# Inverse softmax sums by way of DRAM instead of TensorE transposes, in an attention and feed-forward kernel

## The reference

```python
cq = rms_norm(x @ w_qa.T, q_a_ln_w)
q = (cq @ w_qb.T).reshape(b, s, H, DQ).transpose(0, 2, 1, 3)      # 16 heads of 128 + 64 (rope)
ckv = x @ w_kva.T                                                # 128 latent + 64 rope
kv = (rms_norm(ckv[..., :128], kv_a_ln_w) @ w_kvb.T)...           # k_nope, v
scores = einsum('bhqd,bhkd->bhqk', q_full, k_full) * scale        # causal mask
attn = softmax(scores.astype(float32), axis=-1)
out = einsum('bhqk,bhkd->bhqd', attn, v).transpose(0, 2, 1, 3).reshape(b, s, H * DV) @ w_o.T
x = layernorm(x + out)
x = layernorm(x + x @ (w_ffn * scale_w[:, None]).T + bias)
```

## Time and profile before

| | us |
|---|---|
| median of 3 runs (1714.79 to 1720.11) | 1716.27 |
| the profiled execution, its own time | 1716.44 |
| its span | 1714.7 |
| PE busy | 1679.9 (98%) |
| DVE busy | 1380.5 (81%) |
| ACT busy | 1120.8 (65%) |
| POOL busy | 979.7 (57%) |

### The profile page before, as it was taken

One profiled execution on the slowest core, in us unless ns is written; L12 is line 12 of the kernel. 1 busy time (PEld: TensorE's weight loads), 2 busy tenths in 40 slices (PEclk: granted clock), 3 DMA queues, 4 the chain that ended last, 5 costly groups with the idle time before them and its releaser, 6 DMA issues.

```text
span 1714.7 us, 28541 instructions
## 1 busy us (share of the span) xinstructions
PE 1679.9 (98%) x8789; PEld 1395.8 (81%) x8789; DVE 1380.5 (81%) x2493; ACT 1120.8 (65%) x2128; POOL 979.7 (57%) x937
## 2 busy tenths in 40 slices
PE   7999999999999999999999999999999999999997
PEld 5567888888888888888888888888888888888775
DVE  3665788888888887878788888888888888888984
ACT  3564676666666676666677666766667777676774
POOL 4333465565555555655566555555556665556785
PEclk9999999999999999999999999999999999999999
DMA  7984322212321412223211413123123111111422
GB/s 204 367 330 136 105 68 62 87 56 88 110 80 37 144 36 81 69 80 117 81 62 44 142 50 92 51 80 114 62 66 105 56 57 62 50 44 44 136 92 80
DMA packets 112175, 164.03 MB, mean 96 GB/s; under 512 B 13600, under 2 KB 83488, under 8 KB 109984
## 3 DMA queue, kind: packets, MB, share of 16 engines
q1 hardware_dynamic: 105296, 125.86, 22.9%
q0 software_dynamic: 4864, 16.26, 3.0%
q10 hardware_dynamic: 1872, 20.19, 2.9%
HBM read 101.19 MB, written 61.08 MB: 95 GB/s over the span
## 4 chain that ended last, share of the span: by engine, by line
PE 89%; POOL 3%; DVE 3%; issue 2%; DMA 1%; ACT 1%; DVEq 0%; SPq 0%; ACTq 0%; POOLq 0%
PE rows L1464 35%; PE bank L1494 7%; PE bank L1497 7%; PE bank L1495 7%; PE rows L1527 7%; PE rows L1427 5%; PE bank L1527 3%; PE rows L392 2%; PE rows L1440 2%; PE bank L1427 2%; PE bank L1484 2%; PE bank L1440 1%; POOL split_p L1730 1%; PE rows L1473 1%; PE rows L1505 1%
## 5 line engine op out<-in xcount | busy, mean ns | idle before, releaser
L1730 POOL TENSOR_TENSOR split_p<-pool,split_p 128x512 fp32r<-128x512 f32 x544 | 703.3, 1294 | 503.2 <-ACT split_p L1618 503.1
L1464 PE MATMUL rows<-q_c,key_c 128*128 128x512 f32 x1632 | 477.0, 400 | 1.4 <-DVE top L1858 1.4
L1606 ACT COPY pool<-rows 128x512 f32<-128x512 f32 x480 | 281.8, 587 | 227.3 <-PE rows L1464 226.6
L1858 DVE TENSOR_TENSOR top<-rows,top 128x512 f32<-128x512 f32 x420 | 288.6, 687 | 124.5 <-ACT pool L1606 121.0
L1873 DVE TENSOR_TENSOR pool<-bank,pool 128x512 f32<-128x512 f32 x544 | 369.7, 680 | 19.8 <-PE bank L1484 19.8
L1611 ACT ACTIVATE pool<-pool 128x512 f32<-128x512 f32 x544 | 345.9, 636 | 18.1 <-DVE pool L1873 17.1
L1618 ACT CAST split_p<-pool 128x512 fp32r<-128x512 f32 x544 | 333.2, 612 | 16.7 <-PE bank L1497 16.7
L1464 PE MATMUL rows<-q_pe,key_pe 128*128 128x512 f32 x1088 | 337.1, 391 | 0.4 <-DMA q_pe<-pe_dram 0.4
L1885 DVE TENSOR_TENSOR bank<-bank,pool 128x512 f32<-128x512 f32 x480 | 330.9, 689 | 0.0
L1464 PEld LDWEIGHTS rows<-q_c,key_c 128*128 128x128 f32 x1632 | 288.0, 189 | 50.0 <-DVE top L1858 5.0
L1464 PEld LDWEIGHTS rows<-q_pe,key_pe 128*128 128x128 f32 x1088 | 204.2, 188 | 46.2 <-DMA q_pe<-pe_dram 0.9
(11 more groups left out here) (193 smaller groups left out, 2101.9 us busy)
## 6 DMA issues: line engine op xcount, KB each, us to landing
q_pe<-pe_dram SPq DMA_DIRECT2D x128, 128.0 KB, 2.6
y_dram<-y SPq DMA_DIRECT2D x62, 256.0 KB, 2.1
cq<-cq_dram SPq DMA_DIRECT2D x19, 768.0 KB, 4.9
y<-y_dram SPq DMA_DIRECT2D x48, 256.0 KB, 3.0
pe_dram<-by_sin SPq DMA_DIRECT2D x32, 256.0 KB, 2.1
pe_dram<-by_cos SPq DMA_DIRECT2D x32, 256.0 KB, 2.2
cq_more<-cq_dram SPq DMA_DIRECT2D x10, 768.0 KB, 4.9
table<-table_dram SPq DMA_DIRECT2D x56, 128.0 KB, 2.7
```

Source lines behind the costliest of these rows:

```text
L1464: mm = pe.matmul(by_head(out), k, q, start=(z == 0), stop=(z == 4))
L1606: nc.scalar.copy(slot(n), SCORES[n % N_SCORES]).then_inc(scores_copied, 1)
L1730: nc.gpsimd.tensor_tensor(split_p[:, n % 2, 1, :], slot(n), stored(split_p[:, n % 2, 0, :]), ALU.subtract).then_inc(p_lo, 1)
L1858: nc.vector.tensor_tensor(out, SCORES[n % N_SCORES], slot(number(it, 0)) if t == 1 else out, ALU.max).then_inc(scores_maxed, 1)
```

## The change

`by_transfer(it)` picks 52 of the 64 query tiles: all but the last six and those six others whose next but one tile ends fewer than 8 slots after them (it 1, 5, 17, 21, 33 and 37). For these, `spread_sum` is gone. In its place SyncE stores `inv_sum` to a DRAM row of 512 numbers, head by head (`store_inv`, 128x4 elements, each element on its own in DRAM), waits for the store to land, and loads the row with one DMA onto all 128 partitions (`load_inv`, 128x512 floats), into one of two buffers. `normalise` multiplies by that SBUF row instead of the PSUM bank and moves from one slot after e + 3 to e + 7, `y` from e + 5 to e + 8. The buffers take the room of two ring tiles, so the ring goes from 24 to 22.

```diff
-RING = 24
+RING = 22
...
+def by_transfer(it):
+    return it + 6 < N_ITER and last_value(it + 2) - last_value(it) >= 8
...
-        yield e + 3, USE_AT, ("spread_sum", it)
-        yield e + 5, USE_AT, ("y", it)
+        if by_transfer(it):
+            yield e + 2, COPIES, ("store_inv", it)
+            yield e + 3, COPIES, ("load_inv", it)
+            yield e + 7, READ, ("normalise", it)
+            yield e + 7, READ, ("o_hi", it)
+            yield e + 7, READ, ("o_lo", it)
+            yield e + 8, USE_AT, ("y", it)
+        else:
+            yield e + 3, USE_AT, ("spread_sum", it)
+            yield e + 5, USE_AT, ("y", it)
...
+            def store_inv(it):
+                sp.wait_ge(inv_done, it + 1)
+                sp.dma_start(m.inv_dram[it].rearrange("(h p) -> p h", h=HG), inv_sum[it % 2],
+                             allow_slow_non_contiguous=True).then_inc(inv_stored[TRANSFERS[it] % 2], 16)
+            def load_inv(it):
+                n = TRANSFERS[it]
+                if n >= 2:
+                    sp.wait_ge(normalised, [o for o in TRANSFERS if TRANSFERS[o] == n - 2][0] + 1)
+                sp.wait_ge(inv_stored[n % 2], 16 * (n // 2 + 1))
+                sp.dma_start(inv_rows[:, n % 2, :], m.inv_dram[it].rearrange("(a n) -> a n", a=1).broadcast_to([P, P * HG])
+                             ).then_inc(inv_loaded[n % 2], 16)
...
             def normalise(it):
-                dve.wait_ge(sum_spread, it + 1)
                 dve.wait_ge(out_copied, it + 1)
+                if by_transfer(it):
+                    n = TRANSFERS[it]
+                    dve.wait_ge(inv_loaded[n % 2], 16 * (n // 2 + 1))
+                    nc.vector.tensor_tensor(o_sum[:, it % 2, :], inv_rows[:, n % 2, :], o_sum[:, it % 2, :], ALU.mult
+                                            ).then_inc(normalised, 1)
+                    return
+                dve.wait_ge(sum_spread, 1 + sum(not by_transfer(o) for o in range(it)))
```

More of the change, by code:

```diff
@@ L89, in __init__ @@
         self.small = sb("small", [P, 64])
-        self.pool = sb("pool", [P, RING * 512])
+        self.pool = sb("pool", [P, (RING + 2) * 512])
         self.cq_dram = nc.dram_tensor("cq_dram", (NCH, P, 2 * KR * 512), F32, kind="Internal").ap()
@@ L111, in __init__ @@
         self.cq_loaded = [ctx.enter_context(nc.semaphore(f"cq_loaded{n}")) for n in range(3)]
+        self.inv_dram = nc.dram_tensor("inv_dram", (G * NT, P * HG), F32, kind="Internal").ap()
         self.y_dram = nc.dram_tensor("y_dram", (NT, P, HID), F32, kind="Internal").ap()
@@ L734, in last_value @@
     return VALUE_SLOT[FIRST[it + 1] - 1]
+def by_transfer(it):
+    return it + 6 < N_ITER and last_value(it + 2) - last_value(it) >= 8
+TRANSFERS = {}
+for it in range(N_ITER):
+    if by_transfer(it):
+        TRANSFERS[it] = len(TRANSFERS)
 def window_slot(s, j):
@@ L917, in waits_for @@
         if it >= 2:
-            yield ("spread_sum", it - 2)
+            yield ("normalise", it - 2) if by_transfer(it - 2) else ("spread_sum", it - 2)
+    elif what == "store_inv":
+        yield ("reduce_sum", it)
+    elif what == "load_inv":
+        yield ("store_inv", it)
+        for other in TRANSFERS:
+            if TRANSFERS[other] == TRANSFERS[it] - 2:
+                yield ("normalise", other)
     elif what == "spread_sum":
@@ L922, in waits_for @@
         yield ("copy_out", it)
-        yield ("spread_sum", it)
+        yield ("load_inv", it) if by_transfer(it) else ("spread_sum", it)
     elif what == "o_hi":
@@ L1098, in sem @@
             return ctx.enter_context(nc.semaphore(name))
-        ring = m.pool[:, :].rearrange("p (r n) -> p r n", r=RING)
+        ring = m.pool[:, 0:RING * 512].rearrange("p (r n) -> p r n", r=RING)
         q_c = sb("q_c", [P, 2, HG, 512], F32R)
@@ L1113, in attention_phase @@
         sums = sb("sums", [P, 4, HG])
+        inv_rows = m.pool[:, RING * 512:].rearrange("p (r n) -> p r n", r=2)
         row_sum = [sums[:, b, :] for b in range(2)]
@@ L1159, in attention_phase @@
         sum_spread = sem("sum_spread")
+        inv_stored = [sem(f"inv_stored{n}") for n in range(2)]
+        inv_loaded = [sem(f"inv_loaded{n}") for n in range(2)]
         normalised = sem("normalised")
@@ L1356, in _ @@
                     given["stores"] += at[0] < output_of(DIRECT)
+                elif what == "store_inv":
+                    store_inv(*at)
+                elif what == "load_inv":
+                    load_inv(*at)
                 elif what == "store_pe":
```

## The result

The changed kernel takes 1774.17 us (median of 4 runs, 1767.41 to 1776.97) against 1715.53 before (median of 4 runs too): a ratio of 1.0336, 95% interval 1.0318 to 1.0353. It is 59 us slower; the prediction said 1698 and 1692 to 1706. The profiled execution took 1771.89 us, its span is 1770.1.

A forecast was written before the change was run, and what follows sets the result against it. TensorE, never idle in the attention phase, was taken as the bound: 24.4 us of transposes removed less 6.1 given back is 18.3, from 1716.44 to 1698 us. Forecast range 1692 to 1704, 1692 to 1706 with the first rival.

The forecast's parts named there:

- The gain: On TensorE, 52 query tiles lose their four transposes at 0.47 us each: 24.4 us, 18.3 after what is given back.
- given back: Where TensorE's weight loads already wait for other engines, a quarter of the 52 savings is lost: 6.1 us.
- The ring: Score copies wait for GpSimd's rest 22 tiles before instead of 24; two key tiles, 3.6 us, remain: no cost.
- TensorE's hold on the time: In the attention phase TensorE never stands still, 299.69 of 300 us, so each microsecond of its work removed shortens the span.
- The price of `normalise`: On VectorE, multiplying two SBUF tiles takes 0.69 us instead of 0.68, 52 times, off the bound: nothing.
- the round trip: Store, SyncE wait and load before `normalise`: 7.3 us against 10.9 at the tightest, so covered, price nothing.
- The upper end that I gave the store: SyncE's store of the inverse sums: 5.2 us at most, from loads of 384 single elements.
- the second rival: `normalise` on VectorE waits for late rows in each of the 52; at R = 14.6 us, 1753 us; chance 0.07.
- The distances: Between inverse and `normalise` six key tiles stand in 50 of 52 cases, 10.9 us at the tightest, up to 17.9.
- Late by 4 us they still hit nothing: Loads of `q_pe`, loads and stores of `y` and `cq` behind SyncE's wait, up to 4.3 us, 52 times: cost 0.
- The third rival: Only the store of 512 single elements is slow; at 10 us with a 3.0 us load, 1709 us; chance 0.04.

## Why the prediction was wrong

**The gain was right in kind and a little large.** 24.4 us were to go from TensorE's work, 21.0 went; 6.1 were to be given back, 5.6 were. In all about 14 us against 18.3, shown by the run without DMAs. The ring (1715.21 us) held, and in that run so did TensorE's hold on the time, busy 98%. The price of `normalise` did not: 0.01 us more for each was taken from a row at 148.1 us beside which GpSimd did nothing, and where rows are in time it is 0.31 us more, 16 us of VectorE's time over the 52. What of the missing gain is due to it was not tested.

**The term that failed is the round trip.** The prediction took 4.3 us for the store, from a load of 512 single elements that went the other way, from DRAM to SBUF, and 3.0 us for the load. The store took 10.1 us to the issue of the load in the median, the load 5.0: 15.1 in place of 7.3. The upper end that I gave the store, 5.2 us, came from the same kind of row, a read; no row bounded a scattered write from above, and the end was no bound. That was said of the price ("no row here shows by how much") and not carried into the range.

**The mechanism was the second rival's, at 0.07.** Its own sum, with the measured R of 15.1: 8 x 4.2 + 17 x 2.0 + 6 x 1.5 = 77 us late, so 1716.4 - 24.4 + 77 = 1769 us, where 1772 was measured. That leaves out what is given back; with the 5.6 us of the run without DMAs it is 1775. The distances were right too, 10.8 us at the first query tile, and from 10.9 to 18.4 us between inverse and `normalise` in the run without DMAs. In VectorE's order six subtractions stand between the two in all 52 cases, also in those where the prediction had four and five key tiles. But the rival came to its own 14.6 us with a load of 8.2 and a store of at most 5.2; that the measured 15.1, a store of 10.1 and a load of 5.0, lies so near is luck. The run with nine key tiles in place of six confirms the mechanism from the other side.

The sum is nearer than its parts, though: VectorE waited 103.4 us and not 77, as many round trips were longer than the median, and of what it waited TensorE lost less. Against the run without DMAs TensorE was idle 52.1 us more and busy 18.7 us more with the same matmuls. In six stretches of 34 us together its granted clock was 0.50, with 24.5 us of busy time in them; at the full clock, by my estimate, this work would have taken half, so the lower clock, which the prediction had not thought of, accounts for about 12 of the 18.7 us. The rest is open.

**"Late by 4 us they still hit nothing"** was true of the changed order and wrong as a statement on SyncE's queue. I had looked at `q_pe`; the run with unused DMAs shows `y` behind two waits in a row, 34 us. In the changed order the later `add_y` hides it.

**The third rival** had the slow store and its reason, single writes that take longer, but at up to 10 us with a load of 3.0, and at 0.04. The chance of slower should have been several times as large: everything hung on one operation with no row of its own.

## What to carry to other kernels

When a change rests on a transfer that the trace doesn't contain, the direction counts: a read of the same elements bounds nothing for a write, and the range must reach to where the time would be if it were several times as long. Before moving work off a full engine into a round trip, count what stands in the order between its ends, and lay DRAM out as the source has it, even if the reader must then take a stride: here this turned 59 us lost into 9 won. Price an operand's move from PSUM to SBUF from rows beside which the other engines work as they will in the new place. A wait in SyncE's queue is paid by whatever transfer stands behind it, also if nobody needs the one waited for.

## What was not expected of the hardware

- Single 4-byte writes to DRAM held SyncE 8.8 us for 512 neighbours and 7.1 for 128, 2.6 for 512 at a pitch of 16 bytes, and 1.9 at 64; 128 pieces of 16 bytes side by side held it 1.8.
- VectorE's product of two SBUF tiles, begun while GpSimd was inside a subtraction, ended 0.55 us after it, in 40 of 40 cases of the run without DMAs; with one operand in PSUM it took 0.68 us regardless. In six other cases both began within 0.05 us of each other and VectorE came first: it took its 0.68 us, and GpSimd's instruction 1.79 to 1.85 instead of 1.29.
- A stride of 16 bytes made float32 operations of 128x512 longer on each engine: VectorE's product 0.99 to 1.32 us in the mean and 0.68 to 1.05 at the least, ScalarE 0.59 to 1.10, GpSimd 1.30 to 1.57.
- In or shortly after some of TensorE's waits for late rows its granted clock fell, six times ahead of the last 10 us and not once there in the kernel before or in the run without DMAs; a wait of 3.0 us ahead of the product at 1372.09 us had no such fall. The product at 689.60 us of the changed kernel followed 4.1 us of idle time and took 5.22 us where 2.72 is usual; the stretch 690 to 694.5 had a granted clock of 0.51, the 1.2 GHz level. The timeline, then the stretch (us, PE busy, clock, DMA share, GB/s):

```profile
689.60 5.22 PE L1574 MATMUL rows<-wo,o_t 128*128 128x512 f32 x12 [4.10 <-ACT o_t L1683]
```

```profile
690.00:694.50 4.50, 4.50 (x12) 0.51 0.37 125
```
